# A 1-core gated cross-attention stack: products of the second and third mixtures taken out of their place in TensorE's order

## The reference, cut to what matters

```python
def _L2_ffn_ref(hidden_states, gate_w, w_gate, w_up, w_down):
    scores = jax.nn.softmax(logits, axis=-1)
    topk_w, topk_ids = jax.lax.top_k(scores, TOP_K)
    topk_w = topk_w / (topk_w.sum(axis=-1, keepdims=True) + 1e-20)
    ...
    h = jax.nn.silu(g) * u          # g, u: x times w_gate, w_up of the chosen experts
    out = h @ w_down                # then weighted by topk_w and summed

def _L3_ffn_ref(x, router_w, gate_w, up_w, down_w, shared_gate_w, shared_up_w, shared_down_w):
    ...
    routed = jnp.einsum('enh,ne->nh', y, combine)
    shared = jax.nn.silu(xf @ shared_gate_w) * (xf @ shared_up_w) @ shared_down_w
    return (shared + routed).reshape(B, S, H)
```

## Time and profile before

| | us |
|---|---|
| median of 3 executions | 631.29 |
| lowest and highest | 630.81, 634.93 |
| the profiled execution: its time | 634.09 |
| the profiled execution: span from first to last instruction | 632.3 |
| mean granted TensorE clock of that execution, as a share of full speed | 0.989 |

### The profile page before, as it was taken

One profiled execution on the slowest core, in us unless ns is written; L12 is line 12 of the kernel. 1 busy time (PEld: TensorE's weight loads), 2 busy tenths in 40 slices (PEclk: granted clock), 3 DMA queues, 4 the chain that ended last, 5 costly groups with the idle time before them and its releaser, 6 DMA issues.

```text
span 632.3 us, 16475 instructions
## 1 busy us (share of the span) xinstructions
PE 572.3 (91%) x5475; PEld 291.5 (46%) x5475; DVE 519.3 (82%) x1136; ACT 340.0 (54%) x675; POOL 248.7 (39%) x456
## 2 busy tenths in 40 slices
PE   3899899979878899978999999999999879997997
PEld 2444588726643355532443334333443435563443
DVE  6798886888889778766899999999999886666796
ACT  3878776555545243433555555555655563342654
POOL 3475010312771378861434444344343100325352
PEclk9999999999999999997999999999999899999999
DMA  8600200140000000004366666666566000001110
GB/s 318 215 2 2 69 3 2 34 123 3 3 2 0 3 3 2 3 12 117 115 162 180 180 168 164 175 181 176 161 174 177 6 1 2 2 3 39 30 50 33
DMA packets 34913, 48.91 MB, mean 77 GB/s; under 512 B 6756, under 2 KB 26800, under 8 KB 34472
## 3 DMA queue, kind: packets, MB, share of 16 engines
q1 hardware_dynamic: 34424, 47.40, 26.7%
q10 hardware_dynamic: 432, 0.73, 0.3%
HBM read 47.29 MB, written 0.82 MB: 76 GB/s over the span
## 4 chain that ended last, share of the span: by engine, by line
DVE 43%; PE 40%; ACT 7%; issue 4%; POOL 3%; DMA 1%; DVEq 0%; ACTq 0%; POOLq 0%
PE PS L228 28%; DVE PS L1115 9%; DVE SHARED L1268 5%; DVE SHARED L1792 4%; DVE PS L1128 3%; ACT SHARED L1093 2%; DVE MB L1921 2%; PE PS L2027 2%; ACT SHARED L1064 2%; PE PS L1899 2%; PE PS L2033 2%; DVE PS L1921 2%; DVE STAT L394 1%; DVE XN L410 1%; DVE REC L2041 1%
## 5 line engine op out<-in xcount | busy, mean ns | idle before, releaser
L228 PE MATMUL PS<-XH,UH 128*128 128x512 f16 x232 | 90.1, 388 | 7.4 <-DVE PS L1115 3.4
L1093 ACT ACTIVATE SHARED<-PS 128x512 f16<-128x512 f32 x96 | 57.1, 597 | 72.9 <-DVE PS L1128 68.4
L228 PE MATMUL PS<-XL,UH 128*128 128x512 f16 x232 | 89.6, 386 | 0.0
L228 PE MATMUL PS<-XH,UL 128*128 128x512 f16 x232 | 89.3, 385 | 0.0
L2008 ACT ACTIVATE SHARED<-PS 128x512 f32<-128x512 f32 x96 | 52.1, 595 | 62.5 <-PE PS L228 48.8
L228 PE MATMUL PS<-SHARED,DNH 128*128 128x512 f16 x232 | 69.0, 379 | 2.1 <-DVE SHARED L1268 2.0
L1022 POOL CAST DNH<-DF 128x128 f16<-128x128 f32 x58 | 19.4, 334 | 123.8 <-DMA DF<-in_down 93.1
L1064 ACT ACTIVATE SHARED<-PS 128x512 f32<-128x512 f32 x96 | 57.2, 597 | 19.7 <-PE PS L228 14.7
L1268 DVE TENSOR_TENSOR SHARED<-PS,SHARED 128x512 f16<-128x512 f32 x96 | 62.0, 687 | 6.8 <-ACT SHARED L1093 3.3
L1128 DVE TENSOR_TENSOR PS<-PS,SHARED 128x512 f32<-128x512 f32 x92 | 59.7, 694 | 3.8
L1115 DVE TENSOR_TENSOR PS<-SHARED,PS 128x1024 f32<-128x1024 f32 x46 | 56.5, 1229 | 6.7 <-PE PS L228 0.7
(11 more groups left out here) (345 smaller groups left out, 1276.7 us busy)
## 6 DMA issues: line engine op xcount, KB each, us to landing
SHARED<-w_rows_dram SPq DMA_DIRECT2D x31, 384.0 KB, 3.6
SHARED<-w_rows_dram SPq DMA_DIRECT2D x30, 256.0 KB, 3.9
UF<-in_up SPq DMA_DIRECT2D x58, 128.0 KB, 3.4
SHARED<-w_rows_dram SPq DMA_DIRECT2D x31, 128.0 KB, 2.8
DF<-in_down SPq DMA_DIRECT2D x58, 64.0 KB, 3.0
V<-in_up SPq DMA_DIRECT2D x2, 1024.0 KB, 9.2
SHARED<-in_down SPq DMA_DIRECT2D x4, 512.0 KB
SHARED<-t_values_dram SPq DMA_DIRECT2D x2, 1024.0 KB, 10.4
```

The lines of the kernel that those rows point to most:

```text
L228: last = pe.matmul(dst, l, r, start=start and i == 0, stop=stop and i == len(pairs) - 1)
L1093: act.activation(HHI[:, u, hf, :], bank(4 + hf) if m == 1 else HF[:, hf, :], ACT.Copy).then_inc(sem("e_high"), 1)
```

## The change

In the second mixture, TensorE's up(1) with its wait moves from the head of step 1 to step 0, behind the transposes of the weights and ahead of select(0). 8 fill matmuls come ahead of gate(1) and 6 ahead of the transposes, all into bank 7. VectorE runs gated(1) directly behind gated(0) and ahead of weigh(0). gated(1) now goes into TG instead of HF, and for rounds 0 and 1 the wait for `e_low` ahead of it is gone.

In the third mixture, the gate half of `moe_pe_up` becomes `moe2_pe_gate`. gate(1) of both halves is issued ahead of the turn of the weights, with 3 fill matmuls before it and 2 behind it, into bank 7. Step 1 then issues only its up products. Loads, GpSimd's and ScalarE's lists are untouched.

```diff
--- before.py
+++ after.py
@@ -1026,11 +1026,8 @@
 
         def moe_pe_up(pe, m, c, u, h, hf):
 
-            a = MOE[m]["at"] + c
-            if hf == 0:
-                pe.wait_ge(sem("e_up_ready"), 2 * a + 2)
-            pe.wait_ge(sem("e_act"), 2 * a + hf - 1)
-            products(pe, bank(hf), three(UH[:, u, 0:128], UL[:, u, 0:128], XHh[hf], XLh[hf])).then_inc(sem("e_gate"), 1)
+            if not (isinstance(c, int) and c == 1):
+                moe2_pe_gate(pe, m, c, u, hf)
             beyond(pe, "e_gated", 2 * c + hf - 1)
             products(pe, bank(2 + hf), three(UH[:, u, 128:256], UL[:, u, 128:256], XHh[hf], XLh[hf]))\
                 .then_inc(sem("e_up2"), 1)
@@ -1041,6 +1038,14 @@
             if not (isinstance(c, int) and c == 2):
                 pe.wait_ge(sem("e_hidden"), 2 * c + hf - 5)
             products(pe, bank(4 + hf), [(SEL[:, u, :], CT[:, HALF * hf:HALF * hf + HALF])]).then_inc(sem("e_weight"), 1)
+
+        def moe2_pe_gate(pe, m, c, u, hf):
+
+            a = MOE[m]["at"] + c
+            if hf == 0:
+                pe.wait_ge(sem("e_up_ready"), 2 * a + 2)
+            pe.wait_ge(sem("e_act"), 2 * a + hf - 1)
+            products(pe, bank(hf), three(UH[:, u, 0:128], UL[:, u, 0:128], XHh[hf], XLh[hf])).then_inc(sem("e_gate"), 1)
 
         def moe_pe_down(pe, m, c, u, hf, start=False, stop=False):
 
@@ -1110,8 +1115,10 @@
 
             dve.wait_ge(sem("e_act"), 2 * c + 2)
             dve.wait_ge(sem("e_up1"), 2 * c + 2)
-            beyond(dve, "e_low", 2 * c)
-            dst = HF.rearrange("p i n -> p (i n)") if isinstance(c, int) and c < 2 else bank(4, 2)
+            first = isinstance(c, int) and c < 2
+            if not first:
+                beyond(dve, "e_low", 2 * c)
+            dst = (HF, TG)[c].rearrange("p i n -> p (i n)") if first else bank(4, 2)
             dve.tensor_tensor(dst, SG1[u].rearrange("p i n -> p (i n)"), bank(2, 2), ALU.mult).then_inc(sem("w1_gated"), 1)
 
         def moe1_dve_weigh(dve, c, u, h):
@@ -1120,7 +1127,7 @@
             if isinstance(c, int) and c < 2:
                 for hf in range(2):
                     dve.wait_ge(sem("w1_spread"), 2 * c + hf + 1)
-                    dve.tensor_tensor(bank(4 + hf), HF[:, hf, :], bank(4 + hf), ALU.mult)\
+                    dve.tensor_tensor(bank(4 + hf), (HF, TG)[c][:, hf, :], bank(4 + hf), ALU.mult)\
                         .then_inc(sem("w1_second" if hf else "w1_first"), 1)
                 return
             dve.wait_ge(sem(f"w1_in{u}"), 32 * h)
@@ -1223,11 +1230,16 @@
 
             def step(c, u, h):
                 static = isinstance(c, int)
-                moe1_pe_up(pe, c, u)
+                if not (static and c == 1):
+                    moe1_pe_up(pe, c, u)
+                if static and c == 0:
+                    fill_pe(pe, 7, 8)
                 if not (static and c == CH2 - 1):
                     moe1_pe_gate(pe, c + 1, 1 - u, h + u)
                 if static and c == 0:
+                    fill_pe(pe, 7, 6)
                     moe1_rows_pe(pe)
+                    moe1_pe_up(pe, 1, 1)
                 if static and c < 2:
                     moe1_pe_select(pe, c)
                 if not (static and c == 0):
@@ -1637,6 +1649,10 @@
                 for hf in range(2):
                     moe_pe_up(pe, m, c, u, h, hf)
                 if isinstance(c, int) and c == 0:
+                    fill_pe(pe, 7, 3)
+                    for hf in range(2):
+                        moe2_pe_gate(pe, m, 1, 1, hf)
+                    fill_pe(pe, 7, 2)
                     route_turn_pe(pe, 2)
                 if not (isinstance(c, int) and c == 0):
                     for hf in range(2):
@@ -1681,7 +1697,10 @@
 
             def step(c, u, h):
                 if m == 1:
-                    moe1_dve_gate(dve, c, u)
+                    if not (isinstance(c, int) and c == 1):
+                        moe1_dve_gate(dve, c, u)
+                    if isinstance(c, int) and c == 0:
+                        moe1_dve_gate(dve, 1, 1)
                     moe1_dve_weigh(dve, c, u, h)
                 else:
                     for hf in range(2):
```

## The result

The kernel with the change takes 628.97 us, median of 7 executions (628.42 to 629.40). Beside it the kernel before takes 634.47, median of 7 (630.81 to 636.42). The medians differ by 5.5 us. The ratio of the two sets of executions is 0.9923, interval 0.9896 to 0.9950, which is a saving of 4.9 us, between 3.2 and 6.6. The profiled execution after takes 629.32 us with a span of 627.5, where before had 634.09 and 632.3. So the saving is near the forecast 5.4, and the level is 3.1 us above the forecast 625.9: the median of 631.29 that I subtracted from was too low. The forecast of the time against the profiled execution's own, 628.7, met 629.3.

What follows compares the result with a forecast made beforehand. VectorE's gated products bound the second mixture's loop, TensorE's matmuls the third's; the openings gain by earlier starts. 3.7 + 1.7 = 5.4 us off the median of 631.29 gives 625.9, range 624.3 to 629.3.

Steps and rivals of the forecast that it cites:

- What bounds each loop: VectorE paces the second mixture's loop at 4.18 us a round, TensorE the third's, so earlier starts of these engines stay gained.
- Rival D: Both loops, really paced by transfers or GpSimd, absorb the lead: no gain, 631.3 us; chance 0.07.
- The chain in the second mixture: Second mixture's opening: gated(2) starts near 299.05 instead of 302.72, 3.7 us earlier, 2.6 from the clock, about 1 from reordering and selects.
- The chain in the third mixture: Third mixture's opening: down(0) starts 1.7 us earlier, 3.0 us behind the transposes instead of 4.7, after a 1.1 us wait.
- The clock in the new order: TensorE's granted clock stays at 1.00 through both openings, where it had fallen to 0.50; no row showed this.
- Rival B: Timed executions lack some of the profile's slow stretches, so 1.7 us of the gain is missing: 627.6 us; chance 0.16.
- The range: Median time for 8 in 10, from the forecast's own spread plus two rivals: 624.3 to 629.3 us.
- rival A: Second mixture's opening: clock still falls at the fp32 selects, first gain shrinks from 3.7 to 0.9: 628.7 us; chance 0.14.
- The chances: Whole kernel: forecast 0.60; faster by over 1% 0.17, within 1% 0.81, slower by over 1% 0.02.
- Rival C: Clock falls before up(1) for over 10 us, and at down(0)'s new wait in the third mixture: 632.7 us; chance 0.03.
- its rule on transposes: Skill's Part 4: transposes don't count as clock activity like matmuls, so the clock could still fall around the weights' turn.

Runs made afterwards that it cites:

- e3: Kernel before with fills alone in its idle stretches of both openings, old order kept: 629.84 us, ratio 0.9923 against the kernel before.
- e5: The unchanged kernel before, executed and profiled once more: 633.76 us, median of 12, ratio to itself 0.9989.
- e2: Only the third mixture's part of the change, second mixture as in the kernel before: 634.52 us, ratio 0.9991 against the kernel before.
- e4: The whole change without its 19 fills, so the reordering alone: 629.77 us, ratio 0.9926 against the kernel before.
- after: First profile of the whole change; that execution took 629.32 us, span 627.5, where the kernel before had 634.09 and 632.3.

## Why the prediction was right and where it was wrong

- **What bounds each loop**: right. Rounds of the second mixture stay at 4.18 (281.4 us from gated(2) to the turn before and after), and the third keeps all of its 1.7. Rival D is out.
- **The chain in the second mixture**: right. 10.72 behind the transposes, 10.8 forecast. I put 2.6 on 12 slow matmuls (12 x 0.21 is 2.5) and about 1 on the order and the selects together. The first select pair took 2.91 at the low clock and 1.98 at the upper one, so nearly all of that 1 was clock too. By `e3` and `e5` the clock is 3.33 and the order 0.44: the forecast had the sum right and credited the order with too much, and as the clock's part isn't lost in every execution, that part decides what the timed executions gain.
- **The chain in the third mixture**: right, 3.07. Here the order is worth nothing by itself: fills alone give the same 3.07. The new place of gate(1) does what 13 fills do, keep TensorE busy ahead of the turn.
- **The clock in the new order**: right, 1.00 in every profile of the whole change, in both openings.
- **The step that failed: "That execution is 2.8 above the median of 631.29, so the median should come to 631.29 - 5.4 = 625.9."** The profile was not an unlucky execution; the median was a lucky one. Sets of 7 to 32 executions of the kernel before put it at 633.8 to 635.4, and 634.09 - 5.4 = 628.7 would have stood within 0.3 of 628.97. The row of times was there to warn: 630.81, 631.29 and 634.93 leave a gap of 3.6 between two values and the third. Rival B saw that timed executions may lack a slow stretch, but priced the missing stretch at 1.7, half of 3.4. The second opening's fall measured 3.33 us of the chain. If the executions at 631.29 lacked it, 631.29 - 5.4 + 3.33 = 629.2 (an estimate) was to be expected, near the 628.97. So 5.4 was taken off executions in which, by that estimate, some 2 were to be had.
- **The range and rival A**: 628.97 lies within 624.3 to 629.3, but only because A and B had stretched the range upward, and A's price of 628.7 is near it by luck: its fall at the selects was in no profile of the new order. (A's gated(2) at 301.9 is also 0.8 under 302.72, not 0.9.)
- **The chances**: 0.81 on within 1% and the sentence that 1% is about what a measurement can tell were too coarse. The ratios of the whole change (0.9916 to 0.9925) are within 1% but their intervals end at 0.9954 at most, clear of 1. This step failed too: runs of this size can tell a change of 0.8% from none. The forecast should have said a small gain, clear of the noise.
- **Rival C**: never seen. The 1.0 us of idle ahead of down(0) started no fall in any of the seven profiles with it; the next fall in them came at 625 or later, or not at all.

The Trainium skill's "TensorE: Matmul & The Clock Gate", Part 1, says that how many matmuls run at the low clock differs from run to run of one kernel. I weighed only its rule on transposes. This case's runs agree with the first: the same program with the same idle stretches had 6.5 us at 0.50 in one execution and none in the other.

## What to carry to other kernels

An opening with several idle stretches of TensorE can be a lottery: here the same program lost 3.3 us to the clock in one profiled execution and nothing in another. Judge such a change by the distance between two events in several profiles, and take the base from the group of executions to which the profile belongs. Fill only up to the signal that is waited for, and when an engine is brought forward, look at which other engine its helpers will now meet.

## What the runs showed of the hardware that was not expected

- Idle stretches of 2.3 and 1.6 us ahead of the transposes did not always bring a fall. The old order had one in two of three profiles without fills (before, `e2`; not `e5`), the new order without fills had none in its one (`e4`).
- A fall does not always cost time. The one from 502.6 to 506.0 before the change cost nothing that can be seen: from gated(2) to the turn it was 281.4 us with it and 281.4 in `after` without.
- Clock falls lie at different places in executions of one kernel: at 45 and 124 in the first profile of the whole change, none of them in the second (span 626.6 against 627.5).
- VectorE's low part grew in the mean from 709 to 814 ns when GpSimd's subtraction for the up weights, itself 670 to 840 ns, came to lie beside it, and 16 columns instead of 256 brought it back to 723. It matters which starts first: GpSimd's 128x128 subtraction took 0.92 us behind the start of a low part and 0.43 alone.
